# Recommender tower on one core: ninth selected table, gram in two column tiles, reordered start and last transfers

## The reference

```
e = stack([tbl_f[ids[:, f]] for f in range(26)], axis=1)         # 2048 x 26 x 128
combined = concatenate([dense[:, None, :], e], axis=1)           # 2048 x 27 x 128
inter = einsum('bfd,bgd->bfg', combined, combined)               # 27 x 27 per sample
z = concatenate([dense, inter[:, upper triangle without diagonal]], axis=1)   # 128 + 351
h = concatenate([z, dense], axis=1)                              # 607
h = maximum(h @ W_top1 + b_top1, 0)                              # 512
h = maximum(h @ W_top2 + b_top2, 0)                              # 256
y = h @ W_top3                                                   # 1
```

## Time and profile before

| | us |
|---|---|
| median of 3 runs (lowest, highest) | 397.05 (396.08, 397.63) |
| the profiled execution | 399.06 |
| its span, first to last instruction | 397.3 |
| PE busy in the span | 356.9 (90%) |
| PEld busy | 339.4 (85%) |
| DVE busy | 184.2 (46%) |
| ACT busy | 192.8 (49%) |
| POOL busy | 275.2 (69%) |

### The profile page before, as it was taken

One profiled execution on the slowest core, in us unless ns is written; L12 is line 12 of the kernel. 1 busy time (PEld: TensorE's weight loads), 2 busy tenths in 40 slices (PEclk: granted clock), 3 DMA queues, 4 the chain that ended last, 5 costly groups with the idle time before them and its releaser, 6 DMA issues.

```text
span 397.3 us, 7469 instructions
## 1 busy us (share of the span) xinstructions
PE 356.9 (90%) x2832; PEld 339.4 (85%) x2832; DVE 184.2 (46%) x146; ACT 192.8 (49%) x361; POOL 275.2 (69%) x294
## 2 busy tenths in 40 slices
PE   0476797989999999999999999999699999999996
PEld 0465696979899989999899989999599989999896
DVE  2879770705446334815445344915229155541112
ACT  2345547643564455545465446544355445654520
POOL 5777777777777777777777777777777777776000
PEclk9998999999999999999999999999799999999999
DMA  7976129832734145422643153522625223432220
GB/s 248 289 196 198 47 64 253 201 93 53 188 83 106 54 84 160 108 70 53 195 85 93 53 125 122 123 55 55 191 54 122 56 58 85 88 88 54 43 50 21
DMA packets 62821, 43.30 MB, mean 109 GB/s; under 512 B 51508, under 2 KB 55435, under 8 KB 61778
## 3 DMA queue, kind: packets, MB, share of 16 engines
q1 hardware_dynamic: 53586, 24.16, 24.0%
q0 software_dynamic: 9216, 18.89, 18.2%
HBM read 37.27 MB, written 5.76 MB: 108 GB/s over the span
## 4 chain that ended last, share of the span: by engine, by line
PE 76%; DMA 9%; DVE 5%; issue 4%; SPq 3%; ACT 1%; POOL 1%; DVEq 0%
PE p_gram L344 26%; PE p_sel L324 25%; PE p_mlp L365 9%; PE p_turn L305 6%; PE p_mlp L402 5%; DMA prods<-in_table 5%; PE p_mlp L359 3%; SPq L213 3%; DVE low L577 2%; DMA square<-prods 2%; PE p_mlp L414 1%; DVE h L604 1%; DMA pairs<-square 1%; DMA rows<-in_table,index 1%; DVE prods L574 1%
## 5 line engine op out<-in xcount | busy, mean ns | idle before, releaser
L277 POOL DMA_INDIRECT rows<-in_table,index x288 | 274.5, 953 | 89.5 <-issue 85.9
L594 DVE TENSOR_TENSOR onehot<-ids_all,p_rows 128x2048 fp32r<-128x2048 int32 x64 | 144.8, 2282 | 64.3 <-PE p_sel L324 61.0
L324 PE MATMUL p_sel<-onehot,high 125*128 125x256 f32 x512 | 130.7, 294 | 9.2 <-DVE onehot L594 7.5
L324 PE MATMUL p_sel<-onehot,low 125*128 125x256 f32 x512 | 126.8, 286 | 0.0
L344 PEld LDWEIGHTS p_gram<-feats 128*108 128x108 f32 x1024 | 106.3, 177 | 5.4 <-ACT prods L523 1.4
L344 PE MATMUL p_gram<-feats 128*108 128x104 f32 x1024 | 109.3, 261 | 1.5 <-ACT feats L487 0.9
L324 PEld LDWEIGHTS p_sel<-onehot,high 125*128 125x128 f32 x512 | 99.8, 195 | 10.7 <-DVE onehot L594 8.7
L523 ACT ACTIVATE prods<-p_gram 108x416 f32<-108x416 f32 x128 | 66.7, 521 | 84.0 <-PE p_gram L344 83.5
L324 PEld LDWEIGHTS p_sel<-onehot,low 125*128 125x128 f32 x512 | 99.9, 195 | 0.0
L487 ACT ACTIVATE feats<-p_turn 128x512 f32<-128x512 f32 (+1 forms) x80 | 83.6, 1053 | 30.0 <-PE p_turn L305 30.0
L508 ACT ACTIVATE feats<-p_sel 128x128 f32<-128x128 f32 x128 | 41.9, 440 | 52.4 <-PE p_sel L324 51.7
(11 more groups left out here) (29 smaller groups left out, 74.4 us busy)
## 6 DMA issues: line engine op xcount, KB each, us to landing
ids_all<-in_ids_t SPq DMA_DIRECT2D x8, 1024.0 KB, 6.4
square<-prods SPq DMA_DIRECT2D x64, 87.8 KB
rows<-in_table,index POOLq DMA_INDIRECT x288, 2.5
prods<-in_table SPq DMA_DIRECT2D x8, 448.0 KB
pairs<-square SPq DMA_DIRECT2D x14, 117.0 KB
dense<-in_x_t SPq DMA_DIRECT2D x1, 896.0 KB, 5.7
pairs<-square SPq DMA_DIRECT2D x7, 104.0 KB
wpairs<-in_w_pairs SPq DMA_DIRECT2D x1, 702.0 KB
```

What stands on the lines that cost most here:

```text
L277: pool.indirect_dma_start(out=rows[a][:, f, :], out_offset=None, in_=tables[f], in_offset=bass.IndirectOffsetOnAxis(ap=index[:, (2 * i + a ...
L324: mm = pe.matmul(p_sel[k % 2][:, 0:PAIR], part[k][0:VP, c, :], hot, start=(c == 0 and part is high), stop=(c == VC - 1 and part is low))
L594: nc.vector.tensor_tensor(onehot[k % RING][:, :, :], at, of, ALU.is_equal).then_inc(s_onehot, 1)
```

## The change

Five things are done at once.
- SEL is 9: 17 tables are gathered (34 gathers a pair, the fifth quad has one table), nine are selected.
- The gram of a group of four samples is two products, each of two samples (54 stationary, 52 moving columns), the first written to PSUM partitions 0 to 53, the second to 64 to 117. GB is 8, so a bank holds 8 groups and a tile has 4 banks. ScalarE copies 118 partitions x 416 columns for each. `prods` is half as wide.
- `masked` is in PSUM, in the two banks of `p_gram`. VectorE makes the one-hot of the next table between masking and subtracting. The ids of pair 0 come in three parts, for 2, 3 and 4 tables, the first ahead of table 0, the others behind tables 0 and 1. The ids of pair 1 follow table 4.
- In pair 0 TensorE and ScalarE do the selections of a quad ahead of its turn: three in quad 0, then 1, 2, 1, 2. Layer 2 in the last pair stands in quads 2 and 3, as in the others.
- In the tail SP stores two of the four blocks and reads back two chunks; ScalarE issues the other two of each after its last copy.

```diff
-BLK = 4 * C
-BLKC = 4 * F
-GB = 4
+COLS = 2
+EACH = 4 // COLS
+WIDE = 128 // COLS
+BLK = EACH * C
+BLKC = EACH * F
+GB = 8
 NG = GS // GB
+NH = NG // 2
+RISE = WIDE * (COLS - 1) + BLK
-SEL = 8
+SEL = 9
-STAGES = BLKC * GS // (VC * D)
+STAGES = 2 * BLKC * GS // (VC * D)
+FIRST = 3
+PARTS = (0, 2, 5, SEL)
...
 def selections(q, first, second):
-    n, early = NQ, 0 if first else EARLY if second else 1
-    if not (first or second):
+    if first:
+        starts = [0] + [FIRST + p * (SEL - FIRST) // (NQ - 1) for p in range(NQ)]
+        return range(starts[q], starts[q + 1])
+    n, early = NQ, EARLY if second else 1
+    if not second:
...
-        prods = [sb(f"prods{a}", [128, BLKC, GS]) for a in range(2)]
-        masked = piece[-1]
+        both_prods = sb("prods", [128, 2 * BLKC * GS])
+        p_pair = ctx.enter_context(nc.psum_tensor("p_gram", [128, 2, 512], F32))
+        p_gram = [p_pair[:, k, :] for k in range(2)]
+        masked = p_pair.rearrange("p b (c d) -> p (b c) d", d=D)
...
+        def store_quarter(queue, a, js):
+            for j in js:
+                dst = square.rearrange("(f g) s -> f g s", g=F)
+                lo = a * T + j * GS
+                at, part = WIDE * (j // EACH) + C * (j % EACH), F * (j % EACH)
+                queue.dma_start(dst[:, :, lo:lo + GS], prods[a][at:at + C, part:part + F, :]).then_inc(s_stored[a], 16)
...
+            load_first_ids(0)
             for k in range(SEL):
...
-                if k == 0:
-                    load_ids_all(0, 0)
-                if k == 2:
+                if k < 2:
+                    load_first_ids(k + 1)
+                if k == 4:
                     load_ids_all(1, 1)
...
-            store(NP - 1, 1)
-            read_back(NP - 1, (1,))
+            store(NP - 1, 1, js=(0, 1))
+            read_back(NP - 1, (1,), chunks=(0, 1))
...
                     for k in range(GB):
-                        group = feats[a][:, GB * b + k, :, :].rearrange("d j f -> d (j f)")
-                        mm = pe.matmul(p_gram[b % 2][0:BLK, BLKC * k:BLKC * k + BLKC], group,
-                                       feats[a][:, GB * b + k, :, 1:C], start=True, stop=True)
+                        for tile in range(COLS):
+                            js = slice(EACH * tile, EACH * tile + EACH)
+                            group = feats[a][:, GB * b + k, js, :].rearrange("d j f -> d (j f)")
+                            mm = pe.matmul(p_gram[b % 2][WIDE * tile:WIDE * tile + BLK, BLKC * k:BLKC * k + BLKC], group,
+                                           feats[a][:, GB * b + k, js, 1:C], start=True, stop=True)
...
                 for q in range(NQ):
+                    if first:
+                        for k in selections(q, first, second):
+                            select(i, k, first, second)
                     turn(i, 0, q, first)
...
-                    if q in (2, 3) and not (first or last):
+                    if q in (2, 3) and not first:
                         layer2(i - 1, both, (q - 2,))
-                    if q >= NQ - M2 and last:
-                        layer2(i - 1, both, (q - NQ + M2,))
...
             keep_prods(NP - 1, 1, range(NG))
+            act.wait_ge(s_prods, 2 * NP * NG)
+            store_quarter(act, 1, (2, 3))
+            act.wait_ge(s_stored[1], 64 * NP)
+            load_chunks(act, (1,), (2, 3))
...
+            make_onehot(0, 0, 0, first=True)
             for k in range(SEL):
-                split(k)
-                make_onehot(0, 0, k, first=True)
+                split_high(k)
+                if k + 1 < SEL:
+                    make_onehot(0, 0, k + 1, first=True)
+                split_low(k)
```

More of the change, by code:

```diff
@@ L96, in program @@
         feats = [sb(f"feats{a}", [D, GS, 4, C]) for a in range(2)]
[L97 to L101 removed]
+        both_prods = sb("prods", [128, 2 * BLKC * GS])
+        prods = [both_prods[:, a * BLKC * GS:(a + 1) * BLKC * GS].rearrange("p (c g) -> p c g", c=BLKC)
+                 for a in range(2)]
+        piece = [both_prods[:, k * VC * D:(k + 1) * VC * D].rearrange("p (c d) -> p c d", c=VC)
+                 for k in range(STAGES)]
         pairs = sb("pairs", [KP, NCH, PAIR])
@@ L151, in program @@
         s_ids_all = [sem(f"s_ids_all{b}") for b in range(2)]
+        s_first_ids = [sem(f"s_first_ids{n}") for n in range(len(PARTS) - 2)] + [s_ids_all[0]]
         s_onehot = sem("s_onehot")
@@ L201, in _, with store @@
                     sp.dma_start(dense[:, 0:PAIR], x_t[:, 0:PAIR]).then_inc(s_dense, 16)
-            def store(i, a, first=False):
+            def store(i, a, first=False, js=range(4)):
                 sp.wait_ge(s_prods, (2 * i + a + 1) * NG)
@@ L209, in store, with read_back @@
                     sp.wait_ge(s_pairs, 64 * i)
[L210 to L216, removed]
+                store_quarter(sp, a, js)
+            def read_back(i, tiles, first=False, chunks=range(NCH + 1)):
                 for a in tiles:
@@ L224, in read_back @@
                     sp.wait_ge(s_h1, M1 * i)
[L225 to L233, removed]
+                load_chunks(sp, tiles, chunks)
             def pair(i, b, first=False, second=False, last=False, late=False):
@@ L424, in pair @@
                 for q in range(NQ):
+                    if first:
+                        for k in selections(q, first, second):
+                            select(i, k, first, second)
                     turn(i, 0, q, first)
                     if q < 2 and not (first or second):
-                        gram(i - 1, 1, range(4 * q, 4 * q + 2))
+                        gram(i - 1, 1, range(NH * q, NH * q + (NH + 1) // 2))
                         if q == 0:
                             select(i, 0)
-                        gram(i - 1, 1, range(4 * q + 2, 4 * q + 4))
-                    for k in selections(q, first, second):
+                        gram(i - 1, 1, range(NH * q + (NH + 1) // 2, NH * q + NH))
+                    for k in selections(q, first, second) if not first else ():
                         select(i, k, first, second)
@@ L440, in pair @@
                     if q < 2:
-                        for b in range(4 * q, 4 * q + 4, 2):
+                        for m in range(2 * q, 2 * q + 2):
                             if not first:
-                                layer1(i - 1, b // 2, first=second)
-                            gram(i, 0, (b, b + 1))
+                                layer1(i - 1, m, first=second)
+                            gram(i, 0, range(NH * m // 2, NH * (m + 1) // 2))
                     if first and q < EARLY:
                         select(1, q, second=True)
-                    if q in (2, 3) and not (first or last):
+                    if q in (2, 3) and not first:
                         layer2(i - 1, both, (q - 2,))
@@ L513, in keep_prods @@
                 t = 2 * i + a
-                if first and a == 1:
+                if first:
                     act.wait_ge(s_low, SEL)
@@ L533, in pair @@
                 for q in range(NQ):
+                    if first:
+                        for k in selections(q, first, second):
+                            if k + 2 < SEL:
+                                high_bits(k + 2)
+                            keep_selected(i, k, first)
                     keep(i, 0, q, first)
                     if not (first or second) and q < 2:
-                        keep_prods(i - 1, 1, range(4 * q, 4 * q + 4))
+                        keep_prods(i - 1, 1, range(NH * q, NH * q + NH))
                     if second and q == 0:
@@ L541, in pair @@
                         keep_selected(i, 0)
-                    for k in selections(q, first, second):
-                        if first and k + 2 < SEL:
-                            high_bits(k + 2)
+                    for k in selections(q, first, second) if not first else ():
                         keep_selected(i, k, first)
@@ L549, in pair @@
                     if q < 2:
-                        keep_prods(i, 0, range(4 * q, 4 * q + 4), first=first)
+                        keep_prods(i, 0, range(NH * q, NH * q + NH), first=first)
             for k in range(2):
@@ L580, in make_onehot @@
             def make_onehot(i, b, k, first=False):
-                if k == 0:
+                if first and k in PARTS:
+                    dve.wait_ge(s_first_ids[PARTS.index(k)], 16)
+                elif k == 0:
                     dve.wait_ge(s_ids_all[b], 16 * (i // 2 + 1) if isinstance(i, int) else 8 * (i - b) + 16)
```

30 lines of the change are left out of this document (24 added, 6 removed).

## The result

| | before | after |
|---|---|---|
| median, us | 396.94 (4 runs) | 382.94 (4 runs) |
| profiled execution, its span | 399.06, 397.3 | 383.99, 381.8 |

The ratio is 0.9646 (95% interval 0.9625 to 0.9666): 14 us faster, where 28 were forecast. 369 is 14 us too low, the range held the time. From pair 2 on the kernel went the way of the rival "partly overlapped loads, or drains that do show"; but 9.3 of the 14.7 us between the forecast span and the measured one were lost before pair 2 began.

A forecast was written before the change was run, and what follows sets the result against it. TensorE and GpSimd were taken to bind side by side. Last gram start 348.7 + tail 18.4 = 367.1 us span, 368.9 profiled; median 2.0 lower, drains 1 to 2 back: 369 us, range 362 to 395.

The forecast's parts named there:

- partly overlapped loads, or drains that do show: Rival, 21%: gram above 7.8 us a pair makes TensorE the bound again; time 376 to 394 us.
- What bounds: Whole kernel: TensorE at 44.1 us a pair and GpSimd's gathers at 45.3 stand side by side; both must be shortened.
- Ninth table: TensorE's pair: one more selection, +1.94 us, two turns fewer, -0.25; net +1.7 us a pair.
- Tiled gram: TensorE's pair: a group takes 95 ns instead of 190, so the gram falls from 12.1 to 6.1 us a pair.
- the forecast's middle: Pairs 2 to 7: GpSimd binds from about pair 4, TensorE waits about 3 us a pair; last gram starts at 348.7.
- The mechanism under it: Gram: loads of the two column halves go side by side, so a group takes half, 95 ns.
- Start, VectorE: Startup: first one-hot near 4.5 us, masked copy 1.27, 4.63 us a table; selection 8 ends at 49.3 to 49.6.
- Start, SP: Startup: weight loads still end at 67.1, the tile's store leaves at 67.3, layer 1 starts at 84.4 us.
- Clock falls at each pair's wait: Rival within the partly overlapped range: TensorE's clock falls at each wait, some 1.4 us a fall; time 370 to 371.
- Tail: After the last gram's start: gram and copy save 3.2 us, split stores 1.5; 18.4 us instead of 23.1.
- 0 if the transfers themselves take the time: Tail: lower bound on the gain from splitting the four stores; at best 1.7 us, taken as 1.5.
- Serial loads, slower than before: Rival, 20%: loads or issue go one after the other, deciding from 44 ns an instruction; time 400 us and more.

The follow-up runs named there:

- Experiment 1: The changed kernel with eight selected tables instead of nine, 18 gathered: 389.8 us, ratio to the kernel before 0.9815.
- experiment 2: The changed kernel with the gram untiled, part of its products left out: 531.7 and 530.8 us, against 537.5 and 544.9 before, on chips about 35% slower.
- experiment 7: The changed kernel with SP loading all weights ahead of both stores of pair 0, masked copy still in PSUM: 376.9 us, ratio to before 0.9512.
- experiment 3: The changed kernel with both products of a group written to one column tile: 568.6 us against 537.5 for the kernel before, on chips about 35% slower.
- experiment 4: The changed kernel with four column tiles instead of two: 611.9 us against 544.9 for the kernel before, on chips about 35% slower.
- experiment 6: The changed kernel with weights loaded ahead of both stores of pair 0 and the masked copy in SBUF: 379.3 us, ratio to before 0.956.

## Why the prediction was right in sign and half in size

- **What bounds.** Right: two engines side by side, and both must be shortened. Experiment 1 shows it from GpSimd's side: with eight tables the gathers bind, with nine TensorE does. TensorE's side, nine tables with the gram untiled, has no time at full speed (experiment 2); by its rows a pair would be 42.0 - 8.3 + 12.1 = 45.8 us, an estimate.
- **Ninth table.** +1.7 us a pair stands, by the selection's 1.94 us.
- **Tiled gram: the step that failed in size.** It was put at 95 ns a group, 6.05 us a pair, and mode changes at nothing except in the last pair. The seven runs of a pair measure 0.94 + 0.94 + 1.74 + 4 x 0.94 = 7.4 us. Behind them the next products are late: a selection 2.10 for 1.93, a turn 0.59 for 0.44 three times, the dense product of layer 1 0.63 for 0.45 twice, 1.0 us together. The sum, 8.3 us a pair, is past the 7.8 from which the prediction had TensorE bind again. (Seven runs are 14 mode changes; the prediction counted 16.) So 42.0 us a pair instead of 39.7, and GpSimd's row no longer decides. As the forecast's middle already went at GpSimd's pace, (309.2 - 101.1) / 5 = 41.6 us a pair, this step cost only about 4.5 of the 14.7 us: 1.1 between layer 1 and pair 2 (17.8 us in experiment 7, where layer 1 does not wait, for 16.7 forecast), 1.9 up to pair 7 and 1.5 in it. For 8.3 us the rival's own formula gives about 374 (pair 7 at 312.2, then 40.8, 19.6 and 1.8), so this step alone does not explain 383.
- **The mechanism under it** was right: two tiles load and stream at the same time (experiment 3). The Trainium skill (TensorEngine Tiling (Array Packing), Key Properties) says both that tiles work in parallel and that a change of mode drains the engine; the traces agree, with 54 against 29 ns and some 0.15 to 0.2 us behind each run. That delay also stands behind the products of experiment 3 (0.63 us for the dense product) and is missing behind the undivided ones of experiment 2 (0.45), so it goes with the divided product and not with the second tile. The rule of the Trainium skill that the prediction quoted (TensorE: Matmul & The Clock Gate, section on packing small matmuls), that a load overlaps products only of other rows of the array, doesn't hold here: both tiles use all rows.
- **Start, VectorE.** The pace was forecast at 4.63 us a table and is 4.65, the masked copy at 1.27 and is 1.23. The first one-hot began at 5.87 instead of 4.5, as its ids took 4.57 us to land, and selection 8 ended at 51.3 instead of 49.3 to 49.6.
- **Start, SP: the second failed step.** The weights' issues were taken to end at 67.1 as before. They come behind the store of (0, 0), which moved with the late selection 8 from 56.95 to 59.0, took 6.9 us instead of 5.5 from first to last, and end at 70.6; then the store of (0, 1), out at 70.70 instead of the forecast 67.3, was slow as well. TensorE waited 4.4 us at layer 1, and the clock fell with it, which the forecast had not in its sum. From layer 1 to pair 2 took 21.0 us instead of 16.7. Experiment 7 takes the cause away and gets 4.4 + 3 us back: pair 2 comes 7.6 us earlier, the span of the profiled execution is 7.5 us shorter (374.3 for 381.8), and the median 6.0. This step made 6.5 of the 14.7 us (3.3 up to layer 1 and 3.2 behind it), more than the gram.
- **Clock falls at each pair's wait.** There were no waits for rows, and the clock stayed at 1.00 from pair 2 on. Experiment 1 has the waits, and a mean clock of 0.947.
- **Tail.** The gram and its copy saved 2.9 us, of 3.2 forecast. The split of the transfers, taken at 1.5, brought nothing: from the last copy's end to the stores' landing it is 371.17 - 365.43 = 5.74 us, before 386.92 - 381.18 = 5.74 us. The last issue is 0.8 us earlier and its transfer 0.8 us longer, 4.00 for 3.19. The bound "0 if the transfers themselves take the time" was the right one.
- **Serial loads, slower than before.** This rival is excluded by 29 ns an instruction against the 44 from which it would decide.

## What to carry to other kernels

Where two engines are side by side, price a change at both and find the size of each term at which the bound moves: here 1.3 us more of gram and 1 us of mode changes a pair turned a bound by gathers into one by products. What an edit delays by 2 us at the start can grow by what stands behind it in SP's order, here to a wait of 4.4 us and a fall of the clock that cost 3 more; loads that nothing waits for soon belong where the queue and the DMA engines are idle. And a slower copy into PSUM can be the better one when a faster one holds up another engine.

## What the runs showed of the hardware

- Column tiles, 128 rows, float32: one tile 54 ns for an instruction of 54 loaded and 52 streamed columns (experiment 3), two tiles 27.5 to 29 (the changed kernel), and four tiles 12.5 to 14 with half the columns (experiment 4). A group of four samples takes 216, 110 and about 104 ns; undivided it took 190. At these shapes the gain stops at two tiles.
- Behind each run of divided products the next products come 0.15 to 0.2 us late (2.10 for 1.93, 0.59 for 0.44, 0.63 for 0.45).
- VectorE passes within SBUF (a copy of 0.69 us for 1024 columns, a subtraction of 1.22 us with both inputs there) hold up a gather of GpSimd that starts while they run, by nearly the time they have left: 1.23 to 1.33 us instead of 0.94, once 1.57 and once 1.88 (experiment 6). A gather that started first is not lengthened. With the masked numbers in PSUM the copy takes 1.23 us and neither does.
